# A sum of sign bytes placed directly behind the last aggregate of each layer norm on VectorE

## The reference, cut to what matters

```python
x = x + 0.5 * ffn(layernorm(x), W_fc, W_proj)      # first
x = x + attn(layernorm(x), Wk, Wka, Wv, ...)       # att
x = x + 0.5 * ffn(layernorm(x), W_fc, W_proj)      # second

# ffn: h = relu(x @ W_fc.T)**2;  y = h @ W_proj.T
#      then 5 steps of mem = 0.9*mem + y - reset;  result = (number of spikes) / 5
# attn: keys, values, key_att from h = layer_norm(x)*gamma + beta
#      w = exp(key_att/sqrt(128));  w = w / cumsum(w);  cumsum(w * keys) * values
```

## Time and profile before

| | |
|---|---|
| runs, us | 153.90, 153.68, 153.66 |
| median, us | 153.68 |
| the profiled execution, us | 153.72 |
| its span, us | 151.8 |
| granted PE clock | 1.0 in the whole span |
| busy, us (share) | PE 143.5 (94%), PE weight load 125.9 (83%), DVE 128.0 (84%), ACT 129.3 (85%), POOL 99.5 (66%) |

### The profile page before, as it was taken

How to read it: one execution, slowest core, us unless ns; L and a number is a source line. 1 busy time by engine, 2 the same in 40 slices (tenths; PEclk the granted TensorE clock), 3 DMA queues, 4 the chain that set the end, 5 groups by cost and what they waited for, 6 DMA issues and landing times.

```text
span 151.8 us, 3003 instructions
## 1 busy us (share of the span) xinstructions
PE 143.5 (94%) x943; PEld 125.9 (83%) x943; DVE 128.0 (84%) x436; ACT 129.3 (85%) x254; POOL 99.5 (66%) x142
## 2 busy tenths in 40 slices
PE   5899999999999999999989999799799999999990
PEld 5689898989889888887978989789689798989790
DVE  2795379698799999999989999999999999663674
ACT  3277898999999998969989999699699897979772
POOL 1339209878899918983899898988972946190200
PEclk9999999999999999999999999999999999999999
DMA  4875000000000000000000002000020020210222
GB/s 148 249 189 157 4 2 0 0 0 6 0 0 0 4 4 0 0 0 0 4 0 2 0 0 73 0 2 0 0 69 6 0 69 0 69 59 15 69 67 71
DMA packets 10382, 5.09 MB, mean 34 GB/s; under 512 B 1152, under 2 KB 10240, under 8 KB 10368
## 3 DMA queue, kind: packets, MB, share of 16 engines
q1 hardware_dynamic: 9696, 4.40, 10.1%
q10 hardware_dynamic: 672, 0.52, 1.1%
HBM read 2.82 MB, written 2.10 MB: 32 GB/s over the span
## 4 chain that ended last, share of the span: by engine, by line
DVE 31%; PE 30%; issue 15%; ACT 12%; POOL 8%; DMA 2%; SPq 0%; DVEq 0%; POOLq 0%; ACTq 0%
PE work L954 12%; POOL normed L394 4%; DVE stats L584 4%; ACT signs L502 4%; DVE sign_sum L726 3%; DVE pooled L764 3%; PE hidden L890 3%; PE hidden L894 3%; PE hidden L891 3%; DVE weight_key L747 3%; ACT relu L474 2%; ACT square L479 2%; DMA x_first<-_attn_hidden_states_dram 2%; DVE stats_att L584 2%; POOL rstd L388 2%
## 5 line engine op out<-in xcount | busy, mean ns | idle before, releaser
L954 PE MATMUL work<-proj_t,square 128*128 128x128 f32 x480 | 61.8, 276 | 0.1
L954 PEld LDWEIGHTS work<-proj_t,square 128*128 128x128 f32 x480 | 58.9, 192 | 3.1 <-POOL square L409 0.6
L502 ACT ACTIVATE signs<-work 128x512 uint8<-128x512 f32 x73 | 41.3, 619 | 5.5 <-PE work L954 5.5
L474 ACT ACTIVATE relu<-hidden 128x512 f32<-128x512 f32 x64 | 38.2, 626 | 0.8 <-PE hidden L894 0.5
L479 ACT ACTIVATE square<-relu 128x512 f32<-128x512 f32 x53 | 35.3, 667 | 0.3
L890 PE MATMUL hidden<-in_hi,fc_lo 128*128 128x512 f32 x64 | 27.1, 423 | 0.0
L388 POOL TENSOR_TENSOR rstd<-var_eps,minus_half 128x4 f32<-128x4 f32 x15 | 15.6, 1039 | 17.0 <-DVE neg_mean L595 17.0
L894 PE MATMUL hidden<-in_lo,fc_hi 128*128 128x512 f32 x64 | 25.6, 399 | 0.2 <-DVE in_lo L649 0.2
L891 PE MATMUL hidden<-in_hi,fc_hi 128*128 128x512 f32 x64 | 25.1, 392 | 0.0
L394 POOL TENSOR_SCALAR normed<-x_second,neg_mean,rstd 128x128 f32<-128x128 f32 x32 | 18.8, 599 | 0.8
L394 POOL TENSOR_SCALAR normed_att<-x_att,neg_mean_att,rstd_att 128x128 f32<-128x128 f32 x32 | 18.8, 598 | 0.8
(11 more groups left out here) (117 smaller groups left out, 249.6 us busy)
## 6 DMA issues: line engine op xcount, KB each, us to landing
x_first<-_attn_hidden_states_dram SPq DMA_DIRECT2D x7, 256.0 KB, 3.6
out_dram<-x_out SPq DMA_DIRECT2D x7, 256.0 KB, 2.2
fc_raw<-in_L_ffn_W_fc_dram ACTq DMA_DIRECT2D x1, 256.0 KB, 3.2
x_first<-_attn_hidden_states_dram SPq DMA_DIRECT2D x4, 64.0 KB, 3.1
proj_raw<-in_L_ffn_W_proj_dram ACTq DMA_DIRECT2D x1, 256.0 KB, 3.6
out_dram<-x_out SPq DMA_DIRECT2D x4, 64.0 KB, 1.5
att_raw<-in_L_attn_Wk_dram SPq DMA_DIRECT2D x1, 64.0 KB, 3.0
att_raw<-in_L_attn_Wv_dram SPq DMA_DIRECT2D x1, 64.0 KB, 2.7
```

The source lines that it names most:

```text
L474: nc.scalar.activation(relu[j.lane][:, c, :], bank_of_hidden(j, c)[:], ACT.Relu).then_inc(relu_made[j.lane], 1)
L502: nc.scalar.activation(signs[j.lane][:, k, :], work[j.lane][:], func, bias=bias, scale=scale).then_inc(signs_made[j.lane], 1)
L954: last = nc.tensor.matmul(work[j.lane][:, tokens], square[j.lane][:, c, tokens], proj_t[:, c, :], start=(c == 0 and t == 0), stop=(c == NC ...
```

## The change

The sums 1 and 3 are moved in DVE's queue; no instruction is added or removed. `layer_norm` is split into `layer_stats` (the four `bn_stats` and the four `bn_aggr`) and `layer_args` (the waits and the two reductions). Sum 3 of job i - 1 leaves the end of step i and stands in step i + 1 between `layer_stats` and `layer_args` of the feed-forward norm; there the job is i - 2. Sum 1 leaves its place behind `ff_add` and stands behind the squares and the attention's `layer_stats`, ahead of its `layer_args`. The other engines' queues are as before.

```diff
-            def layer_norm(kind, turn, source):
+            def layer_stats(kind, turn, source):
                 for t in range(NT):
                     nc.vector.bn_stats(...)
                 for t in range(NT):
                     dve.wait_ge(stats_made[kind], NT * turn + t + 1)
                     nc.vector.bn_aggr(...)
+
+            def layer_args(kind, turn):
                 if turn:
                     dve.wait_ge(normed_made[kind], NT * turn)
                 dve.wait_ge(moments_made[kind], NT * (turn + 1))
...
-                        ff_layer_norm(j)
+                        ff_layer_stats(j)
+                for j in feed_forward(i - 2):
+                    ff_sum_sign(j, 3)
+                for j in feed_forward(i + 1):
+                    if j.index > 0:
+                        ff_layer_args(j)
                 for b in attention(i - 1):
                     att_weight_key(b)
...
                 for j in feed_forward(i - 2):
                     ff_add(j)
-                for j in feed_forward(i - 1):
-                    ff_sum_sign(j, 1)
                 for j in feed_forward(i):
                     ff_dve_square(j, 0)
                 for j in feed_forward(i):
                     if not j.is_last:
                         ff_dve_square(j, 1)
                 for b in attention(i + 1):
-                    att_layer_norm(b)
+                    att_layer_stats(b)
+                for j in feed_forward(i - 1):
+                    ff_sum_sign(j, 1)
+                for b in attention(i + 1):
+                    att_layer_args(b)
...
                 for b in attention(i):
                     att_sum(b)
-                for j in feed_forward(i - 1):
-                    ff_sum_sign(j, 3)
                 if i == 0:
                     attention_weights()
```

More of the change, by code:

```diff
@@ L615, in first_layer_norm, with ff_layer_stats @@
                                         negate=True).then_inc(made, 1)
-            def ff_layer_norm(j):
+            def ff_layer_stats(j):
                 if j.layer == "first":
@@ L621, in ff_layer_norm, with ff_layer_args, att_layer_stats, att_layer_args @@
                     dve.wait_ge(x_made["second"], j.batch + 1)
-                layer_norm(j.lane, j.turn, x_of[j.layer][j.batch])
-            def att_layer_norm(b):
+                layer_stats(j.lane, j.turn, x_of[j.layer][j.batch])
+            def ff_layer_args(j):
+                layer_args(j.lane, j.turn)
+            def att_layer_stats(b):
                 dve.wait_ge(x_made["att"], b + 1)
-                layer_norm("att", b, x_of["att"][b])
+                layer_stats("att", b, x_of["att"][b])
+            def att_layer_args(b):
+                layer_args("att", b)
             def first_normalise(j, half):
```

## The result

| | before | after |
|---|---|---|
| median, us | 153.67 | 151.16 |
| lowest and highest of 4 runs, us | 153.65, 153.90 | 151.07, 151.56 |
| profiled execution, us | 153.72 | 151.17 |
| its span, us | 151.8 | 149.3 |

The ratio of the runs is 0.9838, with a 95% interval of 0.9825 to 0.9852: the change makes the kernel 1.6% faster, 2.5 us. Forecast were 151.5 us and a range of 150.9 to 152.9. In the later runs most kernels, the one before included, had some executions that took 1.1 to 1.6 us more, which widens their intervals; the profiled execution of add_covered is such a one and loses 1.2 us between 6.5 and 15 us of its span, ahead of every place compared, and one execution of behind_args (158.52 us, at a lower clock) is left out.

What follows compares the result with a forecast made beforehand. The bound was taken to wander from ACT to DVE to PE, with DVE's gains counting fully until the turn of step 11 at 107.59 us. The terms summed to -2.16 us, giving 151.5 us, range 150.9 to 152.9.

Steps and rivals of the forecast that it cites:

- hole: DVE empty between the fourth aggregate's slot and the first reduction, 0.19 us per norm with this wait; a moved sum fills it.
- (a): Step 2, first attention norm: sum 1, free before, now delays the reductions; +0.10 us, bounds 0 and +0.10.
- (b): 31 to 57 us, ACT full: only ACT's wait in step 5 is won; -0.16 us, bounds 0 and -0.19.
- (c): Step 7: PE's third product no longer waits for in_lo; -0.39 us, bounds -0.25 and -0.39.
- (d): Step 8: POOL's guess_sum follows guess sooner, near_share comes earlier; -0.40 us, bounds -0.15 and -0.45.
- (e): DVE full from near_share of step 8 to the turn of step 11: sums' slots saved; -1.16 us, bounds -0.35 and -1.20.
- (f): Step 14: PE waits less for POOL's square, whose norm DVE finishes earlier; -0.15 us, bounds 0 and -0.42.
- Rival 1: Hole not filled, each reduction waits behind the sum's end: 153.5 us, no change; chance 0.10.
- Rival 2: Sums between aggregates and reductions are held by POOL beside its tiles of normed: 154.8 us, slower; chance 0.08.
- Rival 3: Another bound takes most, near_share of step 8 stays put: about -0.8 to -1.2 us, 152.7 us; chance 0.20.

Runs made afterwards that it cites:

- add_covered: The changed kernel, but in steps 2, 3, 4 and 10 sum 1 stands behind ff_add again: 151.33 us, ratio 0.9838 to the kernel before.
- behind_args: Both sums moved as in the change, but behind the two reductions of their norm: median 156.07 us, ratio 1.0189 to the kernel before.
- sum3_only: The changed kernel with sum 1 back behind ff_add, so only sum 3 moves: 152.02 us, ratio 0.9885 to the kernel before.
- sum1_only: The changed kernel with sum 3 back at the step's end, so only sum 1 moves: 153.05 us, ratio 0.9961 to the kernel before.
- sum1_behind: The changed kernel with only sum 1 behind the reductions of the attention norm: 152.81 us, ratio 0.9907 to the kernel before.
- filler_before: The kernel before plus a scratch two-input addition between aggregates and reductions of each of the 23 norms: 153.95 us, ratio 1.0014.
- pool_in_hole: The changed kernel; in steps 5, 6, 9 to 12 sum 3 and weight_key precede layer_stats, scan pool fills the hole: 151.38 us, ratio 0.9833.

## Why the prediction was right

**The mechanism was right**, and the sites were: a hole of 0.19 us that takes a slot of 0.20, a norm that no longer waits for sign 3, and PE passing the shift on from step 11. Its terms against the trace, each as the difference of two of the shifts above:

| part | predicted | measured |
|---|---|---|
| (a) and (b), up to step 5 | -0.06 | -0.14 |
| (c), to PE's product in step 7 | -0.39 | -0.68 |
| (d), to near_share in step 8 | -0.40 | -0.41 |
| (e), to the turn of step 11 | -1.16 | -1.03 |
| (f), to the contraction in step 14 | -0.15 | -0.29 |
| sum | -2.16 | -2.55 |

The total of the terms is closer than some of them: (a) to (c) and (f) were together 0.51 too small, (e) 0.13 too large.

**(a)** had the right sign and a wrong cause. The reductions of step 2 were 0.01 later (26.73, had 26.72), since the norm started a little earlier; POOL's tiles were longer.

**(c) was the mis-sized term.** It counted only PE's wait for in_lo (0.39), which did go, and held the start of PE's job in step 7 to be unmoved. But PE came to it 0.43 earlier (67.21 instead of 67.64), 0.29 of it new since step 5. Already in step 6 PE waits for DVE: its value product waits for att_add, which stands behind the reductions of the attention norm. Before:

```profile
63.49 0.68 DVE L777 TENSOR_TENSOR x_second<-att_value,x_att 128x512 f32<-128x512 f32 x1
64.23 0.50 PE L890 MATMUL att_value<-att_hi,att_w_lo 128*128 128x512 f32 x1
```

and after:

```profile
63.07 0.68 DVE L785 TENSOR_TENSOR x_second<-att_value,x_att 128x512 f32<-128x512 f32 x1
63.80 0.50 PE L903 MATMUL att_value<-att_hi,att_w_lo 128*128 128x512 f32 x1
```

The product starts 0.05 to 0.06 behind the end of att_add in both (64.17 and 63.75), and so it does in sum3_only, sum1_only, behind_args and sum1_behind. POOL kept up: its last tile of that norm, which PE's turn needs next, came 0.43 earlier too, partly since the tiles before took 2.44 instead of 2.68. I had no term for att_add, and none for POOL running faster when DVE's two-input sums leave its side.

**The hole.** Its 0.19 is right by a loose reading. The 0.29 of the earlier trace rows is not the last three aggregates: it is what all four take behind the end of the last bn_stats (94.56 + 0.86 = 95.42). The starts in the trace, 95.34, 95.42, 95.49 and 95.55, give the same 0.07 a piece.

**(e)** was a little too large: sum 1 of step 8 and in_lo of step 9 lost some of it. In step 9 in_lo starts 1.28 behind the scan pool (84.10 to 85.38) instead of 1.13, waiting for ACT. Step 10's uncovered ff_add cost less than taken: the norm starts 99.21 - 98.40 = 0.81 behind it, not 0.88.

**(f)** took only PE's wait for POOL's square. In step 12 PE also waited less for in_lo and DVE's square: its job from the turn at 116.07 to the next at 124.20 lasted 8.13, now 7.94 (113.81 to 121.75). The wait for the square itself gave 0.1. Its bound of 0.42 starts from 136.50, which no row shows: PE's last product before it starts at 136.38 and takes a slot of 0.23, so PE waited 0.31, and now waits 0.20.

**Rival 1** (hole not filled) fell with filler_before. **Rival 2** (held by POOL) was written off by the mean of 42 sums, and in the changed kernel the sums' mean is 303 ns, so rightly here. But a mean hides the few. None of the 42 had met guess_sum; one had met guess_share in step 4, and ends 0.16 behind it (DVE and POOL, before):

```profile
40.69 0.50 DVE L726 TENSOR_TENSOR sign_sum<-sign_sum,signs 128x256 uint16<-128x256 uint16 x1
39.74 1.29 POOL L437 TENSOR_TENSOR guess_share<-weight_key,guess 128x512 f32<-128x512 f32 x1
```

The mechanism is real: it costs up to 1.08 us a time, decided by some tenths of a us of place. That rival 2 stayed away was in part luck: the argument should have been the distance from sum 3 to guess_sum in the timeline. **Rival 3** didn't come: near_share moved by 1.23.

## What to carry to other kernels

A wait between two dependent instructions of one in-order engine is a slot: put an independent instruction there whose slot is no longer than the hole, and measure the slot from start to start, not by the duration. Before moving an instruction with two SBUF inputs on VectorE, look up what GpSimd runs at the new time, not the average over the old places: a long two-input GpSimd operation just ahead holds it to its end. Look the other way too: GpSimd's tile waits for every two-input instruction that VectorE runs without a gap. And once an engine's queue is full, moving the result that its neighbour waits for only moves the wait, as pool_in_hole did.

## What the hardware showed beyond what was expected

- The hold between DVE and POOL lasts to the end of the other's instruction: a 0.28 us addition takes 0.95 to 1.36 us and ends 0.14 to 0.16 us behind POOL's 1.27 us multiplication; begun 0.07 us before it, it takes 0.28. A bn_stats of the same length with one SBUF input takes 277 to 284 ns in all eight places. Beside POOL's normalising tiles it is the same hold, only shorter, since a tile takes 0.44: in the change the sum at 120.27 takes 0.47 and ends 0.14 behind the tile. POOL pays as well: its tiles took up to 1.67 us in the kernel before and up to 1.51 in the change.
- Dependent neighbours on DVE are not all 0.10 us apart: behind the aggregates it is 0.11 from the recorded end, behind ff_add 99.21 - 99.17 = 0.04.
